# Second experts: GpSimd copies each tile's weight and row number before its scatter

## What is computed

```python
scores = softmax(xf @ gate_w.T); _, idx = top_k(scores + gate_b, 2)
w = take_along_axis(scores, idx)
h = silu((xf @ w1 + b1) * (xf @ w3 + b3))       # per expert, 8 experts, width 176
y = sum over the two chosen experts of w * (h @ w2 + b2)
z = the same form with one shared expert, for every row
x = x + y + z
```

## Time and profile before

| | us |
|---|---|
| median of 3 timed executions | 695.43 (694.6 to 695.74) |
| profiled execution: span from first to last instruction | 763.9 |
| PE busy in the span | 671.5 (88%) |
| VectorE busy | 523.5 (69%) |
| GpSimd busy | 504.9 (66%) |
| ScalarE busy | 415.8 (54%) |

### The profile page before, as it was taken

How to read it: one execution, slowest core, us unless ns; L and a number is a source line. 1 busy time by engine, 2 the same in 40 slices (tenths; PEclk the granted TensorE clock), 3 DMA queues, 4 the chain that set the end, 5 groups by cost and what they waited for, 6 DMA issues and landing times.

```text
span 763.9 us, 21054 instructions
## 1 busy us (share of the span) xinstructions
PE 671.5 (88%) x7092; PEld 546.5 (72%) x7092; DVE 523.5 (69%) x1515; ACT 415.8 (54%) x1158; POOL 504.9 (66%) x837
## 2 busy tenths in 40 slices
PE   8799998888876999999979999888888668788797
PEld 7567666665646999999957776666667568778787
DVE  5489988888663446555358898888886555555556
ACT  5477767654542434444447777656547445555563
POOL 5975788577564678877677778777667635455451
PEclk9899999999997999999979999999989989899999
DMA  5470000001331522343110101111211312222264
GB/s 166 124 305 2 17 27 27 27 30 36 137 99 48 160 70 81 97 127 89 46 36 29 30 26 40 54 37 37 66 34 37 89 51 77 61 75 72 75 232 152
DMA packets 45406, 57.78 MB, mean 76 GB/s; under 512 B 11379, under 2 KB 37142, under 8 KB 44630
## 3 DMA queue, kind: packets, MB, share of 16 engines
q1 hardware_dynamic: 36086, 38.17, 16.6%
q0 software_dynamic: 8640, 17.97, 7.1%
q10 hardware_dynamic: 576, 0.29, 0.1%
HBM read 33.82 MB, written 22.08 MB: 73 GB/s over the span
## 4 chain that ended last, share of the span: by engine, by line
PE 50%; POOL 17%; issue 12%; DVE 8%; ACT 5%; another core or an unknown queue 4%; DMA 2%; SPq 1%; DVEq 0%; POOLq 0%; ACTq 0%
POOL results L1625 9%; PE ptp L1349 8%; PE M L1366 7%; PE ptp L2078 6%; PE S L1326 5%; PE S L2059 5%; PE S L1330 3%; PE ptp L1352 3%; POOL xi L1618 2%; POOL rows L626 2%; PE M L1374 2%; PE M L1418 2%; PE S L2065 1%; SPq L707 1%
## 5 line engine op out<-in xcount | busy, mean ns | idle before, releaser
L626 POOL DMA_INDIRECT rows<-out_rows,posi x128 | 126.9, 991 | 50.1 <-issue 32.1
L806 ACT ACTIVATE pT<-ptp 128x512 f32<-128x512 f32 (+1 forms) x192 | 95.1, 525 | 97.7 <-PE ptp L1349 87.0
L1929 POOL DMA_INDIRECT results<-early,xs x71 | 69.0, 971 | 68.4 <-DVE early L2001 50.9
L1064 DVE TENSOR_REDUCE mx<-S 128x16 f32<-128x1232 f32 x64 | 91.3, 1427 | 18.3 <-PE S L1330 16.4
L1625 POOL DMA_INDIRECT results<-early,xi x71 | 75.9, 1069 | 40.5 <-DVE early L1687 35.1
L1065 DVE TENSOR_TENSOR pr<-S,mx 128x1232 f32<-128x1232 f32 x64 | 92.3, 1442 | 2.2
L1724 PE MATMUL S<-first_w,early 128*128 x568 | 77.2, 279 | 3.0 <-DVE early L1687 1.5
L1714 PE MATMUL S<-early,w1s 128*128 128x128 f32 x568 | 76.9, 279 | 0.6 <-ACT early L1659 0.6
L1366 PE MATMUL M<-pT,vm 128*32 128x128 f32 (+1 forms) x2048 | 74.7, 283 | 1.1 <-ACT pT L806 0.6
L1349 PE MATMUL ptp<-cst,pr 128*128 128x128 f32 x512 | 74.0, 290 | 0.0
L1724 PEld LDWEIGHTS S<-first_w,early 128*128 128x128 f32 x568 | 69.5, 193 | 5.9 <-issue 5.7
(11 more groups left out here) (221 smaller groups left out, 1527.9 us busy)
## 6 DMA issues: line engine op xcount, KB each, us to landing
xs<-rows SPq DMA_DIRECT2D x142, 66.0 KB
first_w<-in_e_W SPq DMA_DIRECT2D x2, 2048.0 KB, 8.2
swap<-results SPq DMA_DIRECT2D x32, 128.0 KB
first_w<-results SPq DMA_DIRECT2D x6, 512.0 KB
rows<-out_rows,posi POOLq DMA_INDIRECT x128
x_res<-in_x SPq DMA_DIRECT2D x1, 1536.0 KB, 8.4
W1r<-in_e_W SPq DMA_DIRECT2D x1, 1536.0 KB, 10.8
out_x<-x_res SPq DMA_DIRECT2D x3, 512.0 KB, 2.7
```

The lines of the kernel that those rows point to most:

```text
L626: nc.gpsimd.indirect_dma_start(rows[:, :], bass.IndirectOffsetOnAxis(posi[:, k, n:n + 1], 0), out_rows[:, ring_slot(groups, n), k, :], Non ...
L806: nc.scalar.activation(pT[0:rows_of, G * r:G * r + count, :], ptp[q % 2][0:rows_of, 0:count, :], ACT.Exp, scale=SCALE)\
L1064: do(V.tensor_reduce(mx[:, :].rearrange("p (g j) -> p g j", g=G), sc, AX.X, ALU.max))
```

## The change

GpSimd gets a step `note(i)` for each tile of the second experts. It copies the tile's weight to `wg` (one column of 128 numbers) and, after a wait for that copy, its place to `xi`, both now with 16 columns. The first eight notes stand ahead of the first scatter; after that `note(i + 8)` stands ahead of `send(i)`, until the last eight scatters, which have none. `note` waits for the tile to be in place and, from tile 16 on, until the scatter that used the same column of `xi` has landed. The scatter takes its places from `xi`, VectorE takes the weight from `wg` and waits for the note in place of the load. SP's wait for result and scatter goes: a buffer is loaded again once PE has turned the old tile and GpSimd has noted it. The counter `xi_copied` is that of the first experts, counted on.

```diff
--- before.py
+++ after.py
@@ -1551,7 +1551,7 @@
     hTp, xTp, yp = banks[0:2], banks[2][:, 0, :], banks[3][:, 0, :]
 
     xs_in = st["xs_in"]
-    xi_copied = sem("xi_copied")
+    xi_copied = st["xi_copied"] = sem("xi_copied")
     xsT_ready, xsT_copied = sem("xsT_ready"), sem("xsT_copied")
     hT_ready, hT_copied = sem("hT_ready"), sem("hT_copied")
     yp_ready, ys_ready = sem("yp_ready"), sem("ys_ready")
@@ -1771,6 +1771,7 @@
     U = 8
     XU = 16
     HU = 4
+    AHEAD = 8
     NU = len(UNITS)
     PIECES = ((0, 8), (8, 16), (16, 24), (24, 28), (28, 32))
     STORES = ((0, 8), (8, 16), (16, 24), (24, 28), (28, 32))
@@ -1786,6 +1787,7 @@
     xsT, cs, hm, hT, w1s = sh["xsT2"], sh["cs"], sh["hm"], sh["hT2"], sh["w1s2"]
     S, ptp = sh["S"], sh["ptp"]
 
+    xi, wg, xi_copied = sh["xi"], sh["wg"], st["xi_copied"]
     xs_in = st["xs_in"] + [sem(f"xs_in{s}") for s in range(8, XU)]
     first_use = [16 * len(range(s, SLOTS, 8)) for s in range(8)] + [0] * 8
     xsT_ready, xsT_copied = sem("xsT_ready"), sem("xsT_copied")
@@ -1878,14 +1880,21 @@
         s, before = i % XU, i - XU
         if i >= XU:
             sp.wait_ge(xsT_ready, before // 2 + 1)
-            sp.wait_ge(ys_ready, before + 1)
-            sp.wait_ge(ys_out[before % U], 16 * (before // U) + 16)
+            sp.wait_ge(xi_copied, places_noted(before))
         at = row_of(sp, i) if row is None else row
         sp.dma_start(xs[:, s, :], rows[bass.ds(at, 128), :]).then_inc(xs_in[s], 16)
 
     def in_place(eng, i):
 
         eng.wait_ge(xs_in[i % XU], first_use[i % XU] + 16 * (i // XU) + 16)
+
+    def weights_noted(i):
+
+        return SLOTS + 2 * i + 1
+
+    def places_noted(i):
+
+        return SLOTS + 2 * i + 2
 
     def results_stored(sp, tiles):
 
@@ -1921,14 +1930,28 @@
 
     def gpsimd(pool):
 
+        def note(i):
+
+            s, before = i % XU, i - XU
+            if i >= XU:
+                pool.wait_ge(ys_out[before % U], 16 * (before // U) + 16)
+            in_place(pool, i)
+            nc.gpsimd.tensor_copy(wg[:, s:s + 1], xs[:, s, WGT:WGT + 1]).then_inc(xi_copied, 1)
+            pool.wait_ge(xi_copied, weights_noted(i))
+            nc.gpsimd.tensor_tensor(xi[:, s:s + 1], xs[:, s, IDX:IDX + 1].bitcast(U32), st["zero"][:, 0:1], ALU.add).then_inc(xi_copied, 1)
+
         def send(i):
 
-            s, place = i % U, xs[:, i % XU, IDX:IDX + 1].bitcast(U32)
-            in_place(pool, i)
             pool.wait_ge(ys_ready, i + 1)
-            nc.gpsimd.indirect_dma_start(results[:, :], bass.IndirectOffsetOnAxis(place, 0), ys[:, s, :], None).then_inc(ys_out[s], 16)
-
+            pool.wait_ge(xi_copied, places_noted(i))
+            nc.gpsimd.indirect_dma_start(results[:, :], bass.IndirectOffsetOnAxis(xi[:, i % XU:i % XU + 1], 0), ys[:, i % U, :], None)\
+                .then_inc(ys_out[i % U], 16)
+
+        for i in range(AHEAD):
+            note(i)
         for i in range(SLOTS):
+            if i + AHEAD < SLOTS:
+                note(i + AHEAD)
             send(i)
 
     def scalar(act):
@@ -1997,8 +2020,8 @@
                 for at, i in enumerate(tiles_of(u)):
                     wait(dve, ys_out[i % U], 16 * (i // U))
                     dve.wait_ge(yp_ready, u + 1)
-                    in_place(dve, i)
-                    V.tensor_scalar(ys[:, i % U, :], yp(u)[:, at, :], xs[:, i % XU, WGT:WGT + 1], None, ALU.mult).then_inc(ys_ready, 1)
+                    dve.wait_ge(xi_copied, weights_noted(i))
+                    V.tensor_scalar(ys[:, i % U, :], yp(u)[:, at, :], wg[:, i % XU:i % XU + 1], None, ALU.mult).then_inc(ys_ready, 1)
             else:
                 b = UNITS[u][1]
                 x_updated(dve, b + 1)
@@ -2160,7 +2183,7 @@
               "oh": sb("oh", [128, 2, 8, E]), "both": sb("both", [128, 8, E], BF16), "pos": sb("pos", [128, 8, E]),
               "carry": sb("carry", [128, CARRIES, E]), "posk": sb("posk", [128, 2, 8, E]),
               "posi": sb("posi", [128, 2, B], U32), "swap": swapb,
-              "xs": sb("xs", [128, 16, RW]), "xi": sb("xi", [128, 8], U32),
+              "xs": sb("xs", [128, 16, RW]), "xi": sb("xi", [128, 16], U32), "wg": sb("wg", [128, 16]),
               "hT": early[:, 0:1024].rearrange("p (a c t) -> p a c t", a=2, c=4),
               "ys": early[:, 1024:2048].rearrange("p (u d) -> p u d", d=D),
               "xsT": early[:, 2048:2432].rearrange("p (u t) -> p u t", t=128),
```

## The result

The changed kernel takes 740.98 us (median of 4 runs, 740.13 to 741.54), the kernel before 695.59 beside it (4 runs, 694.6 to 698.41). The ratio is **1.0646 [1.0613, 1.0678]**: 45.4 us slower. The prediction said 706.3, in 694 to 716. The direction was right, the size four times too small.

The account below looks back on a forecast made before the run. GpSimd, at 1.65 us per scatter with two operations, was taken to become the bound in the second experts' timed runs: 14.5 - 0.5 - 3.1 = +10.9 us on the median of 695.4, so 706.3 us, range 694 to 716.

Parts of the forecast that it names:

- the late answers: In the profiled second experts, PE's results reached waiting engines 2.14 to 3.16 us late; 32.4 us were lost there.
- to discount the profile against the timed runs: The profile's 68.5 us excess was taken as delays that the timed runs hardly have, with PE near 2.45 us per unit.
- GpSimd becomes the bound, through `ys` and VectorE: Second experts: GpSimd needs 112.5 us; VectorE waits for old scatters to land before writing `ys`, and PE waits for VectorE.
- The loads gave nothing: Loads going out up to eight tiles earlier were forecast to gain 0, since no wait of PE ends with a load.
- Period with two: 0.96 + 0.39 + 0.27 = 1.62 us: Time between scatter starts with two operations: scatter, gap with one operation, spacing of a waiting pair; taken as 1.65 us.
- First to last scatter: Second experts: 112.5 us with the change against 98, so the last scatter starts 14.5 us later.
- the stretch before: The timed kernel before, from first to last scatter: 128 us less 30 of the lost time, 98 us.
- the faster start: A scatter starts 0.63 us after VectorE's result starts, not 1.10, giving 0.5 us once.
- Tail: After the last scatter, some 3.1 us of slack before PE uses the last loaded piece of results hide part of the delay.
- A (covered): Rival: the timed runs have the delays too, and GpSimd's 1.65 us fits in 1.83 per step; 695.4 us, chance 0.19.
- B (faster): Rival: scatters directly behind each other cause delays in timed runs, and two operations between end them; 680 us, chance 0.11.
- C: Rival: VectorE's copies hold up both new operations of each note, period 2.37 us; 751 us, chance 0.06.

Follow-up runs that it names:

- e1: The kernel before, unchanged, profiled once more on the chip of the other runs: 696.45 us.
- e7: The kernel before plus a useless copy, a wait for it and an add ahead of each of the first 62 scatters of the second experts: 737.29 us, ratio 1.0612.
- e2: The changed kernel without GpSimd's wait for its own weight copy, both operations kept: 710.87 us, ratio 1.0227.
- e6: The changed kernel reordered to weight copy, scatter, wait for the copy, add of the place: 709.9 us, ratio 1.0218.
- e10: e5 with the scatter's two waits in the other order, VectorE's result first and GpSimd's own copy second: 733.78 us, ratio 1.0527.
- e11: The changed kernel with a third operation per note, a copy of a constant column behind the add, waiting for nothing: 740.09 us, ratio 1.0617.
- e5: The changed kernel with one copy noting place and weight together, then a wait for that copy ahead of the scatter: 706.5 us, ratio 1.0169.
- e4: The changed kernel noting places only; VectorE takes the weight from the loaded row and loads wait for VectorE's result: 700.33 us, ratio 1.0077.

## Why the prediction was wrong in size

**Right: what bounds, and the late answers.** The step that I thought boldest, to discount the profile against the timed runs, is borne out by e1.

**Right: GpSimd becomes the bound, through `ys` and VectorE.** VectorE's 43.7 us of waiting for landings are that path. The loads gave nothing, as forecast, but not because a slow GpSimd could not act through them: with the old loads it does (e7).

**Wrong: "Period with two: 0.96 + 0.39 + 0.27 = 1.62 us".** This is the step that failed. The sum took the gap with one note from one place and the spacing of a waiting pair from another. For the operations it was fair: with both, and without an open wait ahead of the scatter, the period is 1.50 (e2, e6). It left out what the open wait does to the scatter behind it: 0.47 us. No part of its range had room for that: the slower end took 1.74 for the period, and its upper edge of 716 is even more than its terms give (706.3 + 5.6 + 2.4 = 714.3). The trace of the kernel before had a place where all three stood together. GpSimd, line 555, which waits for line 554 just ahead of it, then a note and a scatter:

```profile
352.69 0.35 DVE L1687 TENSOR_SCALAR early<-S,xs 128x128 f32<-128x128 f32 x1 [1.00 <-PE S L1724]
...
352.68 0.20 POOL L555 TENSOR_TENSOR nmr<-negm,rstd 128x4 f32<-128x4 f32 x1
352.83 0.19 POOL L1618 TENSOR_TENSOR xi<-xs,zero 128x1 uint32<-128x1 uint32 x1
353.47 1.05 POOL L1625 DMA_INDIRECT results<-early,xi  x1 [0.45 <-DVE early L1687]
```

There the scatter starts 0.45 us after its note and not 0.16 as in the earlier trace rows. I passed it over because the idle time was put down to VectorE, and most of it would have come from there anyway: 0.63 us from the result's start, as in the earlier trace rows, is 353.32. The last 0.15 us aren't VectorE's. In e1 there are two more such places, at 333.77 and 341.93 us. The scatter starts 0.78 and 0.69 us after VectorE's result and both times 0.80 after line 555, so line 555 with its wait sets it.

The gap between forecast and result, term by term (changed kernel against e1, spans 739.4 - 694.6 = 44.8 us):

- First to last scatter: 136.4 - 93.5 = 42.9 instead of 14.5. Of the 28.4 us, 62 x (1.97 - 1.65) = 19.8 are the period. 4.5 are the stretch before, which I put at 98 and not at 93.5: with all lost time gone it would have been 95.6 by that reading. 4.1 are steps longer than the regular ones, 136.4 - (62 x 1.97 + 8 x 1.27).
- Start: the first scatter begins at 587.4 against 586.5, 0.9 later and not 0.5 earlier. In the thirteen profiles it begins anywhere from 579.5 (e10) to 588.8 (e6), with no order by what stands ahead of it, so neither the eight notes nor the faster start can be read from it.
- Tail: 739.4 - 723.8 = 15.6 us after the last scatter's start, against 694.6 - 680.0 = 14.6. A slack was there, though not read from anything that showed the piece landing. PE first uses the last piece 688.33 - 680.05 = 8.28 us after the last scatter's start in e1, without waiting, and 730.14 - 723.84 = 6.30 after it here, having waited for the load: 2.0 us were hidden. But PE, idle for 2.76 us before, then did its last 28 multiplications at the lower clock level (granted 0.52, so nearly all at 1.2 GHz). They took 6.25 us, and 3.28 at the full clock in e1. That is 3.0 us the other way, a term that the forecast did not have.

PE's start on the last piece, and its busy time and granted clock (the number before the last two) from there to its end:

```profile
730.14 1.22 PE L2107 MATMUL ptp<-first_w,cst 128*128 128x128 f32 x4 [2.76 <-DMA first_w<-results]
...
730.14:736.41 6.27, 6.25 (x28) 6.05 (x28) 0.42 (x1) 0.00 (x0) 0.00 (x0) 0.52 0.58 233
```

42.9 + 0.9 + 1.0 = 44.8. The first term is the failed step and its neighbours; the other two miss the forecast's -0.5 and -3.1 by 1.4 and 4.1.

**Rivals.** A (covered) and B (faster) needed the delays in the timed runs, and fell with e1. C gave 751, which is nearer to the result than my forecast, by luck: what it described happened in part, and cost next to nothing. Line 1941 by itself (ns min/median/max):

```profile
L1941 POOL TENSOR_TENSOR xi<-xs,zero x71: 183/185/387, 582.7 to 712.1; 128x1 uint32<-128x1 uint32 x71
```

The median of 185 ns hides a second group. In the timeline 21 of the 71 adds take 0.23 to 0.39 us. Each of these overlaps a copy of VectorE's (line 2005), and only 2 of the 50 short ones do. The rule of the Trainium skill weighed in the prediction ("SBUF — State Buffer") agrees with that. The prediction read from a median that such a meeting is seldom, which was wrong. It costs next to nothing here because a longer add only fills the queue's 0.50 us, as the lines under e11 show. Of line 1939's copies 5 take 0.23 us or more, one of them 0.99.

**The mechanism, and how far it is shown.** The chains show 0.49 and 0.50 us between the queue's instruction ahead of a scatter and its next one behind it, and 0.19 from there to the scatter's start. An open wait by itself isn't slow: in the changed kernel the add starts 0.08 us after the copy's end. So it is the scatter that needs about 0.5 us of the queue. Normally this is hidden behind the scatter before, and 0.16 us pass from a note to a scatter. It is laid bare when the queue reaches the scatter late, because a wait ahead of it was open: that of an operation (the change, e7, e11) or a second wait of the scatter itself (e10, and results that come late in the kernel before). An open wait that the scatter carries itself costs 0.12 us (e5). The Trainium skill ("Perfetto Trace Analysis", "DMA Instruction — SWDGE (GPSIMD)") draws it so: the instruction is decoded by the sequencer and pushed into a wait queue, where it waits for its semaphores. For an instruction of the sequencer alone ("Sequencer-only Instruction (DRAIN, etc)") it draws the wait in the sequencer itself. The traces of e5 and e10 agree, 0.28 against 0.76 us from the copy to the scatter. In one point they differ from the drawing, which lets the sequencer go on once it has pushed: the change's add carries its open wait, and yet the queue's next instruction runs only 0.03 us after the copy's end. The page gives no time for the decoding. That the 0.5 us are this decoding is argued from the order of the queue's instructions, not shown.

## What to carry to other kernels

Where small operations stand between indirect DMAs on GpSimd, look at what the queue waits for ahead of each DMA, not at the operations: merge them, drop the wait between two that don't depend on each other, or put the wait behind the DMA. Give a DMA's first wait to the event that comes last. And price a sequence by a place of the trace where the whole of it stands together, also where the profile names another releaser for its idle time; a sum of parts from different places leaves out what they do to each other. A median doesn't say how often an operation is held up; its single times do. A profile whose span is far from the timed runs should be read against a second one before slack is counted in it.

## What was not expected of the hardware

- The order of two waits on the same values changes the gap ahead of a scatter from 0.28 to 0.76 us (e5, e10), and the time from 706.5 to 733.8 us.
- A small operation between two scatters costs 0.06 us (a copy of two or four elements) to 0.11 (an add), not its 0.19: the rest lies in the 0.30 us between them. The scatter itself took 0.96 to 0.98 us at the median in kernels that have only float copies between scatters, and 0.99 to 1.01 in those with the integer add (e2, e4, e6, e7, e11, the change), for a reason that is open.
- A GpSimd add of 128 numbers took 0.18 to 0.19 us, and 0.23 to 0.39 in all 21 cases of 71 where it was long, each beside a copy of VectorE's. The period stayed near 1.97 us.
- PE, after 2.76 us without work near the end, did 28 multiplications at a granted clock of 0.52, in 6.25 us where 3.28 were enough at the full clock.
- One profiled execution in fourteen was 68.5 us longer than the timed runs, with PE's answers late by 2 to 3 us. Nothing in the kernel explains it.
